# Layer 1's expert blocks on one Trainium2 core: seven blocks' weights loaded in attention in place of four, three buffers of rounded weights, another order on ScalarE and VectorE, eight result slots

## What is computed

```
logits = x @ router_w.T + expert_bias          # 16 experts
top_w, top_idx = top_k(softmax(logits), 4);  top_w /= sum(top_w)
g, u = x @ gate_proj[e], x @ up_proj[e]        # 256 -> 224 each
out[e] = (silu(g) * u) @ down_proj[e]          # 224 -> 256
x = x + sum over the 4 chosen e of top_w[e] * out[e]
```

## Time and profile before

| what | value |
|---|---|
| runs of the kernel before | median 897.15 us (896.73 to 898.09, 3 runs) |
| the profiled execution, first to last instruction | 896.8 us |
| PE busy | 793.8 us (89%) |
| DVE busy | 572.1 us (64%) |
| ACT busy | 386.3 us (43%) |
| POOL busy | 249.5 us (28%) |
| DMA moved | 158.00 MB, mean 176 GB/s |
| last stage (`sparse_experts`) | from 725.8 us on |

### The profile page before, as it was taken

How to read it: one execution, slowest core, us unless ns; L and a number is a source line. 1 busy time by engine, 2 the same in 40 slices (tenths; PEclk the granted TensorE clock), 3 DMA queues, 4 the chain that set the end, 5 groups by cost and what they waited for, 6 DMA issues and landing times. The chain is left out here.

```text
span 896.8 us, 15300 instructions
## 1 busy us (share of the span) xinstructions
PE 793.8 (89%) x5224; PEld 561.8 (63%) x5224; DVE 572.1 (64%) x1340; ACT 386.3 (43%) x847; POOL 249.5 (28%) x310
## 2 busy tenths in 40 slices
PE   5889888999999999997779989998988878999996
PEld 2445445888998999973245655555555447777774
DVE  3798865643332222234878999999977456777764
ACT  1454544333221111101345566656664237777760
POOL 2334420330000000005532345445532313323330
PEclk8999988999999999999788999999998979999999
DMA  9353551391289999818500001101040169999937
GB/s 337 154 235 130 224 188 36 95 366 50 91 290 377 402 338 323 290 55 213 150 6 2 24 26 36 42 25 51 27 167 15 50 224 314 321 339 320 346 117 251
DMA packets 57104, 158.00 MB, mean 176 GB/s; under 512 B 7180, under 2 KB 36748, under 8 KB 51708
## 3 DMA queue, kind: packets, MB, share of 16 engines
q1 hardware_dynamic: 51700, 141.96, 45.4%
q0 software_dynamic: 5328, 15.08, 4.6%
HBM read 114.20 MB, written 42.81 MB: 175 GB/s over the span
## 5 line engine op out<-in xcount | busy, mean ns | idle before, releaser
L1263 PEld LDWEIGHTS ps<-f_xT,f_rg 128*128 128x128 f32 x920 | 113.4, 192 | 6.0 <-DMA f_rg<-w_routed 2.5
L1263 PE MATMUL ps<-f_xT,f_rg 128*128 128x128 f32 x920 | 113.9, 275 | 2.1 <-DMA f_rg<-w_routed 2.1
L1168 DVE TENSOR_TENSOR f_rhT<-f_gate,ps 128x256 f32<-128x256 f32 (+1 forms) x69 | 25.9, 376 | 117.9 <-ACT f_gate L973 79.8
L2097 ACT ACTIVATE b_PX<-ps 128x512 f32<-128x512 f32 x128 | 72.7, 597 | 43.4 <-PE ps L2332 41.5
L1814 DVE TENSOR_REDUCE b_smax<-ps 128x4 f32<-128x1024 f32 x64 | 77.7, 1214 | 10.7 <-PE ps L2308 10.4
L973 ACT ACTIVATE f_gate<-ps 128x256 f32<-128x256 f32 (+1 forms) x69 | 24.0, 348 | 135.0 <-PE ps L1263 135.0
L2622 POOL DMA_INDIRECT y<-f_ys,f_to x47 | 45.8, 975 | 104.5 <-ACT f_ys L2651 52.4
L1277 PE MATMUL ps<-f_rd,f_rhT 128*128 128x256 f32 x230 | 62.3, 387 | 0.0
L2332 PE MATMUL ps<-b_Q,b_Cx 100*128 100x256 f32 x256 | 55.1, 322 | 6.2 <-ACT b_PX L2097 5.8
L1577 POOL MEMSET b_half<- 128x1 f32 x1 | 0.1, 99 | 212.6 <-POOLq L67 212.6
L2332 PEld LDWEIGHTS ps<-b_Q,b_Cx 100*128 100x128 f32 x256 | 40.8, 201 | 26.8 <-ACT b_PX L2097 11.9
(11 more groups left out here) (337 smaller groups left out, 1894.8 us busy)
## 6 DMA issues: line engine op xcount, KB each, us to landing
f_rg<-w_routed SPq DMA_DIRECT2D x23, 1280.0 KB, 7.6
rows<-a_blank SPq DMA_DIRECT2D x16, 1152.0 KB, 7.0
rw<-w_ffn SPq DMA_DIRECT2D x24, 704.0 KB, 6.1
f_rw<-w_ffn SPq DMA_DIRECT2D x23, 704.0 KB, 6.2
f_rd<-w_routed SPq DMA_DIRECT2D x23, 640.0 KB, 5.5
f_yk<-y SPq DMA_DIRECT2D x8, 512.0 KB, 7.1
f_xs<-rows SPq DMA_DIRECT2D x27, 144.0 KB, 5.4
raw<-w_shared SPq DMA_DIRECT2D x10, 384.0 KB, 4.0
```

What stands on the lines that cost most here:

```text
L1263: mm = nc.tensor.matmul(ps[:, u % 4, k * P:(k + 1) * P], rg[b % R_SLOTS][:, off:off + P], xT[b % 2][:, c, :], start=(c == 0), stop=(c == C ...
L2097: nc.scalar.activation(PX[g % RING][:].rearrange("p c m -> p (c m)"), ps[:, RETS + G_TURN[g] % 2, :], ACT.Exp, scale=XSC).then_inc(turn_re ...
```

## The change

In `decoder_kernel` a buffer `later`, [128, 3 x 1408], is held from `attention1` on. In `attention1` its first 4096 columns are the 16 buffers of gathered rows; once all those are added, SP loads the weights of blocks 4, 5 and 6 there. `sparse_experts` gets these seven weight buffers and makes five more (12 in all), has 14 row slots, three buffers `f_wh`, eight result slots and eight address slots. ACT makes f_wh(0) to f_wh(2) ahead of the loop, and in the loop f_wh(b+3), ahead of f_ys(b-2). DVE makes f_wl(b+2) ahead of pick and address of b. SP's first loads are the rows of blocks 4 to 6, then rows and weights of 7 to 11, then rows 12 and 13.

```diff
+LATE1 = 3
...
+        later = whole.enter_context(nc.sbuf_tensor("later", [P, LATE1 * W1], F32))
+        yg1 = later[:, 0:TILES * TOP0 * D].rearrange("p (t k d) -> p t k d", t=TILES, k=TOP0)
+        rw1 = [r[:] for r in rw1] + [later[:, n * W1:(n + 1) * W1] for n in range(LATE1)]
+        w1_loaded = [nc.alloc_semaphore(f"w1_loaded{n}") for n in range(W_SLOTS1 + LATE1)]
...
-        yg = [[sb(f"yg{t}{k}", [P, D]) for k in range(TOP0)] for t in range(TILES)]
...
-            for n in range(W_SLOTS1):
-                sp.dma_start(rw[n][:], w_ffn[n]).then_inc(w_loaded[n], 16)
+            for n in range(W_SLOTS1 + LATE1):
+                if n == W_SLOTS1:
+                    sp.wait_ge(rows_added, TILES)
+                sp.dma_start(rw[n], w_ffn[n]).then_inc(w_loaded[n], 16)
...
-    W_SLOTS, X_SLOTS, Y_SLOTS, A_SLOTS = 2 * W_SLOTS1, 10, 4, 4
+    FIRST, W_SLOTS, X_SLOTS, Y_SLOTS, A_SLOTS = W_SLOTS1 + LATE1, 12, 14, 8, 8
+    H_SLOTS = 3
...
-        wh = [sb(f"wh{n}", [P, DN], F32R) for n in range(2)]
+        wh = [sb(f"wh{n}", [P, DN], F32R) for n in range(H_SLOTS)]
...
-            for b in range(W_SLOTS1, W_SLOTS):
+            for b in range(X_FIRST1, FIRST):
+                load_rows(b)
+            for b in range(FIRST, W_SLOTS):
+                load_rows(b)
                 load_weights(b)
-                load_rows(b)
             for b in range(W_SLOTS, X_SLOTS):
                 load_rows(b)
...
-                if b >= 2:
-                    act.wait_ge(scored, b - 1)
-                nc.scalar.copy(wh[b % 2][:], rw[b % W_SLOTS][:, 0:DN]).then_inc(wh_ready, 1)
+                if b >= H_SLOTS:
+                    act.wait_ge(scored, b - H_SLOTS + 1)
+                nc.scalar.copy(wh[b % H_SLOTS][:], rw[b % W_SLOTS][:, 0:DN]).then_inc(wh_ready, 1)
...
             high_w(1)
+            high_w(2)
...
                     keep_hT(b - 1)
+                if b + H_SLOTS < BLOCKS1:
+                    high_w(b + H_SLOTS)
                 if b >= 2:
                     keep_y(b - 2)
-                if b + 2 < BLOCKS1:
-                    high_w(b + 2)
...
                     low_x(b + 1)
+                if b + 2 < BLOCKS1:
+                    low_w(b + 2)
                 pick_own(b)
                 address(b)
-                if b + 2 < BLOCKS1:
-                    low_w(b + 2)
```

More of the change, by code:

```diff
@@ L122, in decoder_kernel @@
         rw1 = [whole.enter_context(nc.sbuf_tensor(f"rw1{n}", [P, W1], F32)) for n in range(W_SLOTS1)]
-        w1_loaded = [nc.alloc_semaphore(f"w1_loaded{n}") for n in range(W_SLOTS1)]
+        later = whole.enter_context(nc.sbuf_tensor("later", [P, LATE1 * W1], F32))
+        yg1 = later[:, 0:TILES * TOP0 * D].rearrange("p (t k d) -> p t k d", t=TILES, k=TOP0)
+        rw1 = [r[:] for r in rw1] + [later[:, n * W1:(n + 1) * W1] for n in range(LATE1)]
+        w1_loaded = [nc.alloc_semaphore(f"w1_loaded{n}") for n in range(W_SLOTS1 + LATE1)]
         xs1 = [whole.enter_context(nc.sbuf_tensor(f"xs1{n}", [P, ROW1], F32)) for n in range(X_FIRST1)]
         x1_loaded = [nc.alloc_semaphore(f"x1_loaded{n}") for n in range(X_FIRST1)]
-        attention1(nc, w_attn1, ctx_lhs, blank_ctx, blank_values, lam, bias1, X, K, KR, ps, ctx_dram, y0_dram, dest0, wk0, rows1_dram, w_ffn1, rw1, w1_loaded, eb1, rb1,
+        attention1(nc, w_attn1, ctx_lhs, blank_ctx, blank_values, lam, bias1, X, K, KR, ps, ctx_dram, y0_dram, dest0, wk0, rows1_dram, w_ffn1, rw1, yg1, w1_loaded, eb1, rb1,
                    own1, xs1, x1_loaded)
@@ L1326, in routed_experts, with attention1 @@
     end_program(nc, semaphores)
-def attention1(nc, w_attn, ctx_lhs, blank_ctx, blank_values, lam, bias, X, K, KR, ps, ctx_dram, y_dram, y_dest, wk, rows_dram, w_ffn, rw, w_loaded, eb, rb, own, xs,
+def attention1(nc, w_attn, ctx_lhs, blank_ctx, blank_values, lam, bias, X, K, KR, ps, ctx_dram, y_dram, y_dest, wk, rows_dram, w_ffn, rw, yg, w_loaded, eb, rb, own, xs,
                x_loaded):
@@ L1580, in gather @@
                 for k in range(TOP0):
-                    pool.indirect_dma_start(yg[t][k][:], None, y_dram, bass.IndirectOffsetOnAxis(ap=y_dest[:, k, t:t + 1], axis=0)
+                    pool.indirect_dma_start(yg[:, t, k, :], None, y_dram, bass.IndirectOffsetOnAxis(ap=y_dest[:, k, t:t + 1], axis=0)
                                             ).then_inc(gathered[t], 16)
@@ L1704, in add_rows @@
                 for k in range(TOP0):
-                    ins = nc.vector.scalar_tensor_tensor(out=X[:, t, :], in0=yg[t][k][:], scalar=wk[:, k, t:t + 1], in1=X[:, t, :],
+                    ins = nc.vector.scalar_tensor_tensor(out=X[:, t, :], in0=yg[:, t, k, :], scalar=wk[:, k, t:t + 1], in1=X[:, t, :],
                                                          op0=ALU.mult, op1=ALU.add)
@@ L2522, in sem @@
             return semaphores[-1]
-        rw = rw + [sb(f"rw{n}", [P, W1]) for n in range(W_SLOTS1, W_SLOTS)]
-        w_loaded = w_loaded + [sem(f"w_loaded{n}") for n in range(W_SLOTS1, W_SLOTS)]
+        rw = rw + [sb(f"rw{n}", [P, W1])[:] for n in range(FIRST, W_SLOTS)]
+        w_loaded = w_loaded + [sem(f"w_loaded{n}") for n in range(FIRST, W_SLOTS)]
         xs = xs_first + [sb(f"xs{n}", [P, ROW1]) for n in range(X_FIRST1, X_SLOTS)]
@@ L2582, in load_weights @@
                     sp.wait_ge(down_done, b - W_SLOTS + 1)
-                sp.dma_start(rw[b % W_SLOTS][:], w_dram[expert]).then_inc(w_loaded[b % W_SLOTS], 16)
+                sp.dma_start(rw[b % W_SLOTS], w_dram[expert]).then_inc(w_loaded[b % W_SLOTS], 16)
             def load_rows(b):
@@ L2681, in low_w @@
                 dve.wait_ge(wh_ready, b + 1)
-                nc.vector.tensor_tensor(wl[b % 2][:], rw[b % W_SLOTS][:, 0:DN], wh[b % 2][:].bitcast(F32),
+                nc.vector.tensor_tensor(wl[b % 2][:], rw[b % W_SLOTS][:, 0:DN], wh[b % H_SLOTS][:].bitcast(F32),
                                         ALU.subtract).then_inc(wl_ready, 1)
@@ L2744, in gate_up @@
                     at = slice(c * GU, (c + 1) * GU)
-                    nc.tensor.matmul(ps[:, b % 4, 0:GU], xh[b % 2][:, c, :], wh[b % 2][:, at], start=(c == 0), stop=False)
+                    nc.tensor.matmul(ps[:, b % 4, 0:GU], xh[b % 2][:, c, :], wh[b % H_SLOTS][:, at], start=(c == 0), stop=False)
                     nc.tensor.matmul(ps[:, b % 4, 0:GU], xh[b % 2][:, c, :], wl[b % 2][:, at], start=False, stop=False)
-                    mm = nc.tensor.matmul(ps[:, b % 4, 0:GU], xl[b % 2][:, c, :], wh[b % 2][:, at], start=False, stop=(c == C - 1))
+                    mm = nc.tensor.matmul(ps[:, b % 4, 0:GU], xl[b % 2][:, c, :], wh[b % H_SLOTS][:, at], start=False, stop=(c == C - 1))
                 mm.then_inc(scored, 1)
```

## The result

The changed kernel takes 882.53 us in the median of 4 runs (879.11 to 884.61), the kernel before, run beside it, 896.94. The ratio is 0.9828, with a 95% interval of 0.98 to 0.9856: faster by 1.4 to 2.0%. Timed again in five rounds it is 883.61 to 898.15, ratio 0.9833 (0.9813 to 0.9852). Direction and mechanism held; the gain, 14.4 us between the medians and 15.4 by the ratio, was 1.6 to 2.7 us larger than forecast.

The account below looks back on a forecast made before the run. Layer 1's expert blocks alternated between short and long steps because DVE waited for rounded weights and result landings. Span 896.8 less 12.9 plus 0.1 gave 884.0, plus 0.35 to the runs' median 884.4 us; range 882 to 889.5.

Parts of the forecast that it names:

- Parts 1 and 2: Last stage, ACT and DVE: third f_wh buffer and new orders turn long steps into short ones; alone not the whole gain.
- the 12.9 us of the sum: Last stage's 44 steps: the 22 long ones exceed 2.72 by 12.9 us, all saved; some 1.3 from landings alone.
- part 3: Eight result slots in the last stage: 16.3 us of tolerance against a median landing of 5.7; address waits go.
- A: Forecast, chance 0.74: steps of 2.69 to 2.75 give 1.3 either way, small terms up to 1.5 more: 883 to 887.
- Part 4: Twelve weight and fourteen row slots: no gain, but cover for rounding ahead; eight would leave 6.7 us against a landing's 6.1.
- Parts 5 to 7: Early loads in attention, ramp of blocks 0 and 1, added waits and semaphores: nothing to 0.3, nothing to 0.9, 0.1 taken.
- part 7: Four more waits on SP and PE before the last loads, twelve more semaphores: nothing to 0.4, 0.1 us taken.
- The tail: From block 46's first matmul to the kernel's end: 27.8 us, unchanged.
- rival B: DMA becomes the bound in the last stage, weights 2.8 us late: 887 to 892, chance 0.12.
- E: More outstanding loads and scattered results hinder each other, the DMA rate falls: slower, 905 at 291 GB/s, chance 0.03.
- My stock argument: Last stage's DMA, 40.6 MB until block 46's weights: even at 346 GB/s down by 848, wanted after 849.5.
- Rival D: PE's own work becomes the floor as the latency chain shrinks: 0.14 a step, 6 us less, 878, chance 0.03.

Follow-up runs that it names:

- the second profile of before: The kernel before, unedited, timed and profiled once more: median 898.03 us, ratio 0.9991, loop 134.59.
- the fastest kernel: The changed kernel with the rows taken one block further ahead on PE, ACT and DVE: 873.88 us, ratio 0.9729 to the kernel before.

## Why the prediction was right or wrong

**The cause of the long steps: right.** The prediction named two, rounded weights that come late and landings that come late, both on DVE ahead of f_h. Eight result slots alone left the alternation (22 long steps, DVE's wait for f_wh doubled), two buffers in the changed kernel, with ACT's order put back as well, brought 142.91, and ACT's old order with three buffers cost nothing (119.05). With the third buffer alone the regular alternation is gone and 11 long steps by landings are left; with eight result slots and DVE's old order (119.04) these go too, and with both new orders and four slots (120.38) all but two.

**Parts 1 and 2: right in sum, the split was not made.** With three buffers and eight result slots neither new order does anything: the loop is 119.05 with ACT's old one, 119.04 with DVE's. The orders matter where only four result slots stand beside the third buffer; there the two together are worth 7 us of loop. The smallest set that this points to, the third buffer and eight result slots with nothing else, was not run. That parts 1 and 2 alone would not bring it all was right, but they bring 11.1 of 15.0 us: I counted landings that would stand, and not that the address had moved behind f_wl with half a microsecond of room.

**The step that failed: the 12.9 us of the sum, and in it what part 3 takes away.** I wrote in part 2 that some 1.3 us is in the three steps that waited for a landing alone, and took the long steps' 12.9 us, counted in one execution, as the kernel's. That term was sized too small, by two errors. First, the landings cost a varying amount: the second profile of before has a loop of 134.59, and the result slots alone are worth 4.0 us (1.5 to 6.6) over the runs, where I had 1.3. Second, the short step to which the long ones fall is 2.70 and not 2.72: the forecast's loop is 119.6, the measured ones are 118.86 and 119.15, so 0.5 to 0.8 more. Part of it can be seen between Silu and f_h, 0.39 in the changed kernel (776.62 less 776.23) and 0.43 in the earlier trace rows; the rest no row explains. With the loops as measured the sum reads 132.54 to 134.59 less 118.86 to 119.15, 13.4 to 15.7. How the 1.6 to 2.7 us of excess divide between the landings, the short steps and the 2 us outside the loop that the profiles can't tell stays open.

**The sum's frame: wrong.** I had set the profiled span 0.35 below the median as if that were a constant of the measurement. A run's time lies 1.8 to 2.0 above its own span, so the profiled execution was about 1.5 above the median of the runs, and its loop was nonetheless the shorter of two. One profile can't tell which part of an execution is typical. The range's low end, 882, lies 2.4 below the forecast: 1.3 for the steps, and 1.1 for which A gives no reason. With the 2.05 us by which the two loops of before differ it would have reached to about 880.

**Part 4: wrong as a need.** Weight landings take 5.6 to 6.0 in the changed kernel, and with eight slots, where they take 5.9 to 6.0, the 6.7 us cover them and no load was waited for. Slots beyond eight are spare here.

**Parts 5 to 7: nothing against them.** The added wait costs nothing, blocks 0 and 1 take 8.04 us together before and after, and the kernel without early loads has the same loop. A term as small as part 7's 0.1 no run can tell. The tail was said to stay at 27.8; it is 29.5 in the changed kernel's first profile and 28.0 in its second, 27.5 to 29.6 over all kernels and 27.5 and 27.8 in the two profiles of before. Two kernels with the added waits have 27.7 and 27.8, so no cost of the waits shows in it.

**DMA, rival B and E: no danger.** The stage moved 371 GB/s, and when rows were taken further ahead 411 over 20 us. The Trainium skill's bound of about 358 GB/s for a core (DMA: Bandwidth & Descriptors, "Where 436 GB/s comes from") doesn't agree with this program, which runs on one core and moved 371, 394 and 411 in three kernels; the measurement decides. My stock argument was not put to the test, as DMA never fell behind. Results landed in 5.0 us in the median, 5.5 in the fastest kernel, far from 16.3.

**Rival D** had the right idea (PE's own work lies below the chain) and the wrong condition: nothing in this change ends the chain through f_xl. Taking the rows further ahead does, and pays 9 to 10 us (ratio 0.9729 in place of 0.9833), more than D's 6: D had 0.14 a step, the run shows 0.18, and some 2 us come from blocks 0 and 1.

## What to carry to other kernels

Where steps of a loop alternate between two lengths, look on the late engine for an operation that came early enough in one block and too late in the next, and follow it back: here one more buffer in front of it ended the alternation. Look for the second cause that the first one hides, too: the buffer alone brought 4.9 us, more result slots alone 4.0, and only together with a remedy for the landings did the buffer bring 11 to 15. A wait that stands in front of a critical operation in an engine's queue costs far more than one behind it: 19.6 us of waits for landings ahead of f_h stood beside a loop 8.5 us longer, 9.1 us of them behind f_wl beside one 1.2 us longer. Either move such a wait or give it slots; here both together brought little more than one. Take the size of a wait that depends on DMA landings from more than one profile, and compare the profile's own time with the runs before you subtract from it.

## What the runs showed that I had not expected

The core's DMA moved 411 and 406 GB/s in two stretches of 20 us, with weights, rows and scattered results mixed, where 346 at a share of 0.99 had looked full: the share is no measure of what is left (why, no run shows). In the changed kernel 371 GB/s read as 1.00 and in the one without early loads 394 as 1.02. With two buffers the pair of steps shared its delay as 3.10 and 3.39; DVE waited for rounded weights in all 44 blocks there, as it did in the kernel before with eight result slots, where the steps are 2.73 and 3.23. So a loop's pattern alone doesn't tell how many waits it has. And with the rows taken further ahead the clock rose within block 1, at the latest 3.8 us after block 0's first matmul, where in the changed kernel it stayed low nearly up to block 2, 8.0 after; that it was the missing gap of PE that did it, no run shows.
